# Shared-key attention in a four-layer kernel: results transposed in their own PSUM bank, scores in one ring of three banks

## The reference

```python
qh = q.reshape(B, S, KV, G, D).transpose(0, 2, 3, 1, 4)     # KV = 8, G = 4, D = 16
kh = k.reshape(B, S, KV, D).transpose(0, 2, 1, 3)           # k = v = ctx_512
vh = v.reshape(B, S, KV, D).transpose(0, 2, 1, 3)
scores = jnp.einsum('bkgsd,bktd->bkgst', qh, kh) * scale
attn = jax.nn.softmax(scores, axis=-1)
out = jnp.einsum('bkgst,bktd->bkgsd', attn, vh)
x = x + out.transpose(0, 3, 1, 2, 4).reshape(b, s, E)
```

## Time and profile before

| what | value |
|---|---|
| time before, median of 3 runs | 3645.82 us (3643.61 to 3662.2) |
| the profiled execution's own time | 3620.35 us |
| its span on the core | 3618.6 us |
| the two shared-key stages' steps, first to last | 1617 to 1980 us and 2828 to 3194 us |
| PE busy over the span | 3045.3 us (84%) |
| DVE busy | 2256.6 us (62%) |
| ACT busy | 1744.9 us (48%) |

### The profile page before, as it was taken

The page is one execution under the profiler, slowest core; times in us unless marked ns, Lnnn a source line. Parts: engine busy times, 40 slices in busy tenths (PEclk is TensorE's granted clock), DMA queues, the critical chain, the costliest instruction groups (busy, mean ns, idle before and its releaser), DMA issues. The chain is left out here.

```text
span 3618.6 us, 54338 instructions
## 1 busy us (share of the span) xinstructions
PE 3045.3 (84%) x15486; PEld 2098.8 (58%) x15488; DVE 2256.6 (62%) x3833; ACT 1744.9 (48%) x3082; POOL 545.1 (15%) x1148
## 2 busy tenths in 40 slices
PE   4389997799843999658997798999897899979998
PEld 2167885655622888523332587888785333338886
DVE  5876445588352333479995544666556899845555
ACT  5652223355222555337777433666434577754443
POOL 2320000045403000121111310222121011100000
PEclk8689998899966999859999899999998799989999
DMA  4444445875513333343220442667543322102223
GB/s 141 168 137 148 139 139 175 275 176 147 198 59 129 107 109 104 105 123 97 82 59 20 155 163 95 226 240 243 176 148 101 104 81 62 37 30 95 93 93 116
DMA packets 240799, 460.89 MB, mean 127 GB/s; under 512 B 57413, under 2 KB 73925, under 8 KB 240115
## 3 DMA queue, kind: packets, MB, share of 16 engines
q1 hardware_dynamic: 207314, 342.59, 30.6%
q0 software_dynamic: 22480, 96.23, 7.8%
q10 hardware_dynamic: 10864, 20.45, 1.5%
HBM read 342.73 MB, written 113.77 MB: 126 GB/s over the span
## 5 line engine op out<-in xcount | busy, mean ns | idle before, releaser
L1831 DVE TENSOR_REDUCE at_maxima<-psum 128x1 f32<-128x512 f32 (+1 forms) x768 | 620.4, 859 | 39.1 <-PE psum L1739 33.2
L1812 ACT ACTIVATE at_probs<-psum 128x512 f32<-128x512 f32 x1024 | 528.7, 604 | 206.3 <-PE psum L1755 206.3
L1755 PE MATMUL psum<-at_qT,at_kT 50*128 50x512 f32 x1024 | 372.6, 452 | 75.0 <-ACT at_probs L1812 54.9
L1739 PE MATMUL psum<-at_kT,at_qT 48*128 48x512 f32 x1024 | 387.3, 483 | 12.0 <-DVE at_maxima L1831 9.3
L1755 PEld LDWEIGHTS psum<-at_qT,at_kT 50*128 50x128 f32 x1024 | 169.7, 188 | 365.2 <-ACT at_probs L1812 242.6
L1768 PE MATMUL psum<-at_probs,at_vals 128*32 128x512 f32 x2048 | 277.0, 613 | 0.0
L728 PE MATMUL psum<-ffn_w_hi,ffn_hid_hi 128*128 128x512 f32 x768 | 270.9, 393 | 2.7 <-ACT ffn_hid_hi L776 2.7
L486 PE MATMUL psum<-ident,n_normed 128*128 128x128 f32 x512 | 99.2, 360 | 191.3 <-ACT n_normed L449 128.6
L587 ACT ACTIVATE ffn_w_hi<-ffn_w_raw 128x512 fp32r<-128x512 f32 x262 | 161.5, 633 | 157.6 <-PE psum L733 101.2
L595 DVE TENSOR_TENSOR ffn_w_lo<-ffn_w_raw,ffn_w_hi 128x512 fp32r<-128x512 f32 x262 | 176.4, 685 | 77.5 <-ACT ffn_w_hi L587 77.3
L733 PE MATMUL psum<-ffn_w_hi,ffn_hid_lo 128*128 128x512 f32 x768 | 206.3, 390 | 8.4 <-DVE ffn_hid_lo L834 8.4
(11 more groups left out here) (399 smaller groups left out, 6944.2 us busy)
## 6 DMA issues: line engine op xcount, KB each, us to landing
ffn_w_raw<-in_stream SPq DMA_DIRECT2D x262, 256.0 KB, 2.7
ffn_w_hi<-quantized SPq DMA_DIRECT2D x66, 512.0 KB, 3.5
ffn_w_hi<-quantized SPq DMA_DIRECT2D x65, 256.0 KB, 3.1
at_qT<-q_hi SPq DMA_DIRECT2D x256, 64.0 KB, 2.3
ffn2a_w_raw<-in_shared2a SPq DMA_DIRECT2D x26, 512.0 KB, 3.6
qz_raw<-in_stream SPq DMA_DIRECT2D x16, 768.0 KB, 4.8
quantized<-qz_quant POOLq DMA_DIRECT2D x16, 768.0 KB, 3.8
gathered<-zeros SPq DMA_DIRECT2D x1, 12288.0 KB
```

The costliest lines, as they stand in the source:

```text
L1739: mm = pe.matmul(score[n % 4][:, :], qT[r][half(par, USED), jj, t * P:(t + 1) * P], kT[r][half(par, USED), :], start=True, stop=True)
L1755: pe.matmul(scoreT[turn_of(n)][:, :], kT[r][half(h % 2, USED + 2), t * P:(t + 1) * P], qT[r][half(h % 2, USED + 2), h // 2, :], start=True ...
L1812: act.activation(probs[n % RING][:, :], scoreT[turn_of(n)][:, :], ACT.Exp, scale=factor).then_inc(exped, 1)
L1831: dve.tensor_reduce(maxima[g % 2][:, h:h + banks, t], scores, AX.X, ALU.max).then_inc(maxed, 1)
```

## The change

Bank 7 now takes the transposes too: U writes over the result that ACT has just copied away (`turn = room.tiles(7)`). The three banks 4 to 6 form one ring that runs on from group to group, so that each T waits for the exponential three places before it and for nothing else. What waited for bank 4, 5 or 6 to come free of U now waits for bank 7: R0 of a step waits for `finish` of the group before. The blocks are set elsewhere: U behind n = 6 instead of 7, R0 and R1 behind n = 9 and 12 instead of 7 and 11; R2 stays behind n = 15, R3 of the group before behind n = 3. `probs` has 16 buffers instead of 8. `finish` stands one reduction earlier on DVE. On SP six of the 12 loads stand between `send_max` and `put_max`. No arithmetic is added or left out.

```diff
-    RING, SLOTS, LEAD, AHEAD = 2 * H, 8, 3, 6
+    RING, SLOTS, LEAD, AHEAD = PAIRS, 8, 3, 6
...
-    LAST, VALUES, MOVE, RES = 3, (7, 11, 15), 3, 7
+    LAST, VALUES, MOVE, RES = 3, (9, 12, 15), 3, 6
...
-        turn = room.tiles(4 + (RES + 1) % TURNS)
+        turn = room.tiles(7)
...
-        def turn_of(n):
-
-            return (n if n <= RES else n + 1) % TURNS
+        def bank_of(g, n):
+
+            return scoreT[(PAIRS * g + n) % TURNS][:, :]
...
             for s in range(GROUPS):
                 if s + PUT < GROUPS:
                     send_max(s + PUT)
+                if s + AHEAD < GROUPS:
+                    load(s + AHEAD, (0,))
+                if s + PUT < GROUPS:
                     put_max(s + PUT)
                 if s + AHEAD < GROUPS:
-                    load(s + AHEAD)
+                    load(s + AHEAD, (1,))
...
-                if n < 2:
-                    pe.wait_ge(exped, PAIRS * g + n + 1)
-                elif n > 2:
-                    pe.wait_ge(exped, PAIRS * g + (n + 1 if RES < n < RES + TURNS else n))
-                if n == RES + TURNS and g > 0:
-                    pe.wait_ge(finished, g + 1)
+                if PAIRS * g + n >= TURNS:
+                    pe.wait_ge(exped, PAIRS * g + n - TURNS + 1)
...
                 if t == 0:
                     pe.wait_ge(vals_kept, g + 1)
-                    if g > 0:
-                        pe.wait_ge(res_moved, g)
+                    pe.wait_ge(finished, g + 1)
...
                     if n == RES and s > 0:
                         pe.wait_ge(res_moved, s)
-                        pe.wait_ge(exped, PAIRS * s + n + 1)
                         turn_results()
```

More of the change, by code:

```diff
@@ L1672, in spill, with load @@
                     sp.dma_start(dst.rearrange("(c p) t -> p c t", p=P)[:, :, part], src[:, :, part].bitcast(F32)).then_inc(spilled, DMA)
-            def load(g):
+            def load(g, pars=(0, 1)):
                 b, n = g // PER, g % PER
@@ L1679, in load @@
                     sp.wait_ge(spilled, 2 * DMA * (b + 1))
-                for par in range(2):
+                for par in pars:
                     for i, src in enumerate((q_hi, q_lo, q_hi)):
@@ L1748, in scores_T @@
                     pe.wait_ge(put[r], PUTS * DMA * (g // SLOTS + 1))
-                if n < 2:
-                    pe.wait_ge(exped, PAIRS * g + n + 1)
-                elif n > 2:
-                    pe.wait_ge(exped, PAIRS * g + (n + 1 if RES < n < RES + TURNS else n))
-                if n == RES + TURNS and g > 0:
-                    pe.wait_ge(finished, g + 1)
-                pe.matmul(scoreT[turn_of(n)][:, :], kT[r][half(h % 2, USED + 2), t * P:(t + 1) * P], qT[r][half(h % 2, USED + 2), h // 2, :],
+                if PAIRS * g + n >= TURNS:
+                    pe.wait_ge(exped, PAIRS * g + n - TURNS + 1)
+                pe.matmul(bank_of(g, n), kT[r][half(h % 2, USED + 2), t * P:(t + 1) * P], qT[r][half(h % 2, USED + 2), h // 2, :],
                           start=True, stop=True).then_inc(scoredT, 1)
@@ L1762, in results @@
                     pe.wait_ge(vals_kept, g + 1)
-                    if g > 0:
-                        pe.wait_ge(res_moved, g)
+                    pe.wait_ge(finished, g + 1)
                 for h in range(H):
                     n = t * H + h
-                    pe.wait_ge(exped, 2 + PAIRS * g + n + 1)
+                    pe.wait_ge(exped, PAIRS * g + n + 1)
                     pe.matmul(res[h * OW:(h + 1) * OW, :], vals[g % 2][:, t, :], probs[n % RING][:, :],
@@ L1800, in _ @@
         def _(act):
-            act.sem_inc(exped, 2)
             def move_res(g):
@@ L1811, in _ @@
                     act.wait_ge(valued, PAIRS * s + n + 1)
-                    act.activation(probs[n % RING][:, :], scoreT[turn_of(n)][:, :], ACT.Exp, scale=factor).then_inc(exped, 1)
+                    act.activation(probs[n % RING][:, :], bank_of(s, n), ACT.Exp, scale=factor).then_inc(exped, 1)
                     if n == MOVE and s > 0:
```

## The result

The changed kernel takes 3612.34 us (median of 6 runs, 3606.99 to 3620.76), the kernel before beside it 3644.72 us (median of 6). The ratio is 0.9899, 95% interval 0.9872 to 0.9927: faster by 0.7 to 1.3%. The forecast was 3622 with a range of 3596 to 3643; the measured time lies inside it.

The account below looks back on a forecast made before the run. PE, DVE and ACT were taken to pace each other, with none alone the bound. Steady steps 12, last steps 7 and SP's order 4.5 sum to 23.5 us, taking 3645.8 to 3622, range 3596 to 3643.

Parts of the forecast that it names:

- The steady step: Mid-stage steps with scores and reductions, 28 in each of two stages: 11.21 to 11.0 us, 12 us saved.
- The walk: One step followed through PE, DVE and ACT by spacings read from the earlier profile; gave a step of 11.0 us.
- R0's wait: In each steady step R0 waits for `finish` to release the shared bank: 0.77 us, priced at nothing.
- The last steps: Last three steps of each stage, without S or reductions: 11.19 to 9.91 us, 7 us saved in both stages.
- SP's order: Six loads ahead of the read-back shorten idle at the stages' starts: 4.5 us saved, between nothing and 6.6.
- the 2.8: Time by which SP comes sooner to its next send, with six loads hidden in the wait before the read-back.
- The delay of the read-back behind the six loads: At step 3, read-back completes only after the loads; could give back 2.8 us, making the sum 19.
- no long idle at step 3: Sign that the forecast is right: PE's idle of 1.4 or 2.7 us at the stages' step 3 is gone.
- Rival 1: Steady step doesn't move because R0's wait makes the loop longer: 3632 to 3639 us; chance 0.25.
- Rival 2: DVE runs without gaps in steady steps: 45 to 67 us less, 3579 to 3601; chance 0.12.
- Rival 3: Slower: late read-backs of maxima hold up T0; nine late steps make it 3669 us; chance 0.07.

Follow-up runs that it names:

- e9: Changed kernel with `finish` one reduction earlier on DVE, blocks left behind n = 9, 12 and 15; 0.9922 of the kernel before, step 10.97 us.
- e3: Changed kernel with `finish` one reduction later on DVE, where it stood before; 0.9994 of the kernel before.
- e5: Changed kernel run again unchanged, as a second profile; 0.9921 of the kernel before.
- e6: Changed kernel with result blocks behind n = 9, 11 and 14 and `finish` one reduction earlier on DVE; 0.9845 of the kernel before.
- e7: Changed kernel with result blocks behind n = 9, 11 and 14, `finish` left in place; 0.9906 of the kernel before.
- e1: Kernel before with only SP's load order changed, six of 12 loads between `send_max` and `put_max`; 0.9989 of the kernel before.
- e4: Kernel before run again unchanged, as a second profile and measure of noise; 0.9999 of the kernel before.
- e8: Changed kernel with result blocks back behind n = 7, 11 and 15; 1.0228 of the kernel before.

## Why the prediction was right

- **The steady step.** Forecast 11.0 from 11.21; it is 10.97. The walk's places hold one by one: U at 3.51 (3.52), T7 at 4.09 (4.11), R0 at 5.95 (6.08), T10 at 6.95 (7.07), DVE's gap 0.82 (0.83) at S13. `finish` started 0.07 sooner than in the walk, and R0 followed its end within 0.10 instead of 0.15; that is most of R0's 0.13. The term was 12 and is 56 x 0.245 = 13.7.
- **R0's wait, the price of the shared bank.** Priced at nothing, and shown: without it (e9) the step stays 10.97; made 0.6 longer (e3) it sets the step, 11.35. In length it is less than forecast: R0 is held back 0.57 (e9), not 0.77. The rule of the Trainium skill (PSUM — Partial Sum Buffer, "PSUM bank collisions raise a hardware error") that a bank being read is not written does shape this kernel, but as a due time for `finish`, not as a cost. Every run here keeps the rule, so none puts it to the test.
- **The last steps.** Forecast 9.91 each; they take 9.96 and 9.95. The term of 7 stands: per stage two steps are 1.22 shorter and the last is 1.20 shorter up to its last T, 7.3 in both stages, of which 0.3 is given back until the last U.
- **SP's order.** 4.5 was taken between 0 and 6.6. The stages' starts gave 5.2, the 26.2 less 13.7 and 7.3. Layer 3's stage gained 5.4 behind its first step and lost 1.4 in that one; other profiles vary by as much there (12.56 to 14.53). SP did not win all of the 2.8: from the send of group 2 to the read-back of group 3 it takes 21.1 and 20.1 in the two stages, where it took 22.8 and 22.6, so 1.7 and 2.5 less. In layer 2's stage the wait between send and read-back of group 3 even grew, from 5.38 to 7.94; counted from the first issue of the spill ahead of it, it is 9.0 against 8.0. Why is not shown. The delay of the read-back behind the six loads, priced at up to 2.8, did not show. SP's queue and PE's first T of step 3, layer 2's stage, before and after:

```profile
1645.31 1.14 SPq L1692 DMA_DIRECT2D tops<-at_across  x1
1650.69 2.53 SPq L1703 DMA_DIRECT2D at_qT<-tops  x4
```

```profile
1645.61 1.10 SPq L1692 DMA_DIRECT2D tops<-at_across  x1
...
1653.55 2.53 SPq L1703 DMA_DIRECT2D at_qT<-tops  x4
...
1657.49 0.49 PE L1754 MATMUL psum<-at_qT,at_kT 50*128 50x512 f32 x1 [0.35 <-DMA at_qT<-tops]
```

  T0 comes 3.9 behind the first read-back's issue here and came 4.0 and 3.8 behind it before. The last of the six loads was issued at 1652.43, and such loads land 1.8 behind their issue (median in this stage), so they had landed before the last read-back was due; how a longer load would act is not tested. One sign of the prediction, no long idle at step 3, held in the first profile and not in the second (e5: 1.14).
- **The rivals.** Rival 1 is what e3 is: R0's wait 1.12, step 11.35. Its 0.9994 is above the rival's sum, for that had no slow steps in it. Rival 2 (DVE without gaps) did not come with this change; e6 shows what it needs, R1 and R2 one pair sooner and `finish` one reduction earlier, both at once (e7 and e9 have one each and gain nothing). The stated range reaches over a quarter of rival 2's 3579 to 3601, not half. Rival 3 did not come: at no step was a read-back over 1.2 late in the two profiles of the changed kernel.
- **The sum.** 23.5 forecast, 26.2 in the profiles' stages; 32 by the medians of the first comparison, 24 by those of e5, 28 by those of e9, whose steps are the same. 26.2 of 3644.7 is a ratio of 0.9928, just outside the first interval (0.9872 to 0.9927) and inside the others. So the three terms and their causes are shown, and the rest of the first comparison's 32 is not explained by them. Whether the timed runs of before lose a little more than its profile does, for instance in slow last steps as in e1 and e4, was not measured and stays open.
- **What no run tells apart.** The new banks with the blocks in their old places lose (e8). No run has the blocks in their new places with the old banks, so what the places alone would gain is not shown. Nor does any run change the number of `probs` buffers alone.

## What to carry to other kernels

When three engines pace each other, a busy share (DVE's 93% here) doesn't tell what a reordering gives; follow one period through all of them with the spacings read from its rows, and ask at each wait which engine would have been ready instead. Six kernels whose periods were written down that way beforehand came within about 0.1 us of them. A wait that a change adds can cost nothing as long as another wait behind it ends later anyway (R0's 0.57, as e9 shows), and costs once it is longer (0.6 more makes 0.38 a step in e3). Two edits that gain nothing alone (e7, e9) gained 0.56 us a step together (e6).

## What was not expected of the hardware

Gaps on PE can cost more than their own length. Behind an idle 1.12 in front of R0 the clock fell in 5 of 56 steps of e3, behind 1.37 in 22 of 56 steps of e8 (granted clock 0.51, the level of 1.2 GHz, in the three microseconds from 1705), and behind 0.52 in no steady step of the changed kernel. Each time the step was 1.2 to 1.5 us longer, once 2.4. Behind late read-backs it fell for idles of 2.15 to 3.59 and for one of 1.35 (e6), and not for 1.37 in the kernel before. The last steps, which have fewer matmuls, ran slow in one stage each of e1, e4 and e8, and in none of the profiles with the new banks and the later blocks. What decides in which of equal steps the clock falls stays open.
